# Value products by halves of the queries, placed after each of the two heads' scores

## The reference, cut to what matters

```
scores = jnp.einsum('bhqd,bhkd->bhqk', q, k) / SCALING
att = jax.nn.softmax(scores, axis=-1)
out = jnp.einsum('bhal,bhlv->bhav', att, v)
```

## Time and profile before

| | us |
|---|---|
| median of 3 runs (lowest, highest) | 983.62 (983.3, 984.05) |
| profiled execution, its own time | 983.9 |
| its span | 982.1 |
| TensorE busy with matmuls | 882.3 |
| VectorE busy | 792.7 |
| ScalarE busy | 663.7 |

### The profile page before, as it was taken

The page is one execution under the profiler, slowest core; times in us unless marked ns, Lnnn a source line. Parts: engine busy times, 40 slices in busy tenths (PEclk is TensorE's granted clock), DMA queues, the critical chain, the costliest instruction groups (busy, mean ns, idle before and its releaser), DMA issues. The chain is left out here.

```text
span 982.1 us, 14337 instructions
## 1 busy us (share of the span) xinstructions
PE 882.3 (90%) x5188; PEld 319.8 (33%) x5188; DVE 792.7 (81%) x1568; ACT 663.7 (68%) x728; POOL 314.5 (32%) x450
## 2 busy tenths in 40 slices
PE   6879999999999999999999999999989989757985
PEld 3312322222243233322332242322322313136863
DVE  4598879898979878899888879889799788265765
ACT  5128778787877787878877868788677768901110
POOL 4041010005424414139443423255243232822113
PEclk9769999999999999999999999999999989988998
DMA  5631010310320203101411022004310001240001
GB/s 143 105 45 39 16 53 16 73 41 10 90 61 13 93 12 70 38 13 55 89 61 56 12 39 59 23 7 105 91 56 14 11 13 31 85 172 23 1 1 64
DMA packets 52375, 49.08 MB, mean 50 GB/s; under 512 B 17504, under 2 KB 43696, under 8 KB 51920
## 3 DMA queue, kind: packets, MB, share of 16 engines
q1 hardware_dynamic: 51680, 46.91, 19.4%
q0 software_dynamic: 384, 1.05, 0.3%
q10 hardware_dynamic: 240, 0.20, 0.2%
HBM read 18.06 MB, written 9.17 MB: 28 GB/s over the span
## 5 line engine op out<-in xcount | busy, mean ns | idle before, releaser
L1331 DVE TENSOR_REDUCE mx<-ring 128x1 f32<-128x512 f32 x1024 | 633.9, 680 | 110.3 <-PE ring L1038 109.6
L873 ACT ACTIVATE prob<-sc,unscale 128x1024 f32<-128x1024 f32 x512 | 539.1, 1113 | 85.2 <-PE sc L1056 83.9
L1038 PE MATMUL ring<-kp,qp 48*128 48x512 f16 x1024 | 299.4, 395 | 43.5 <-DVE mx L1331 22.5
L1070 PE MATMUL obank<-prob,vaug 128*32 128x512 f32 x2048 | 276.1, 612 | 0.7 <-ACT prob L873 0.6
L1038 PEld LDWEIGHTS ring<-kp,qp 48*128 48x128 f16 x1024 | 74.1, 93 | 361.4 <-DVE mx L1331 301.3
L1056 PE MATMUL sc<-qp,kp 64*128 64x512 f16 x1024 | 167.9, 381 | 14.0 <-ACT prob L873 13.3
L644 POOL TENSOR_TENSOR parts<-qkf,parts 128x1024 f16<-128x1024 f32 x14 | 29.9, 2134 | 209.6 <-ACT parts L803 209.6
L1056 PEld LDWEIGHTS sc<-qp,kp 64*128 64x128 f16 x1024 | 50.4, 95 | 92.3 <-ACT prob L873 83.9
L631 POOL TENSOR_TENSOR hid<-hid,b 128x512 f32<-128x512 f32 x24 | 30.2, 1270 | 110.9 <-ACT hid L827 110.9
L639 POOL TENSOR_TENSOR yA<-yA,sums 128x512 f32<-128x512 f32 x15 | 19.0, 1269 | 131.1 <-DMA sums<-reciprocal_scratch 131.1
L1070 PEld LDWEIGHTS obank<-prob,vaug 128*32 128x32 f32 x2048 | 40.5, 108 | 61.5 <-issue 58.4
(11 more groups left out here) (221 smaller groups left out, 749.2 us busy)
## 6 DMA issues: line engine op xcount, KB each, us to landing
x_sb<-x SPq DMA_DIRECT2D x7, 1024.0 KB, 6.0
kp<-parts SPq DMA_DIRECT2D x48, 128.0 KB, 4.4
qp<-parts SPq DMA_DIRECT2D x93, 64.0 KB, 5.5
out<-hid SPq DMA_DIRECT2D x4, 1024.0 KB, 5.3
yA<-oT SPq DMA_DIRECT2D x124, 32.0 KB
sums<-reciprocal_scratch SPq DMA_DIRECT2D x31, 128.0 KB
x_scratch<-x SPq DMA_DIRECT2D x3, 1024.0 KB, 4.5
qp<-mp SPq DMA_DIRECT2D x128, 2.0 KB
```

What stands on the lines that cost most here:

```text
L873: nc.scalar.activation(prob[:, e % 2, 2 * a:2 * a + 2, :].rearrange("p g n -> p (g n)"), sbuf2[a][:, :], ACT.Exp, scale=unscale[:, 0:1]).t ...
L1038: nc.tensor.matmul(dst[:, :], qp[rows, qh, h, qt * P:(qt + 1) * P], kp[rows, h, kh * HALF:(kh + 1) * HALF], start=True, stop=True).then_in ...
L1070: ins = nc.tensor.matmul(obank[i * VW:(i + 1) * VW, :], vaug[:, b % 2, kt, c0:c0 + VW], prob[:, v % 2, i, :], start=(kt == 0), stop=(kt == ...
L1331: nc.vector.tensor_reduce(mx[:, u % 2, n:n + 1], src[:, :], AX.X, ALU.max).then_inc(rv_free, 1)
```

## The change

The value product is cut by query columns into two halves of 256. Each half is four heads' products with the same weights. Half 0 stands after scores(0), and scores(1) moves behind the second couple of max products, in front of half 1. The waits of the value product are on half 0, its signal `s_av` on half 1. The start flag of the bank is on half 0 of kt = 0 alone.

```
-                def value_product(v):
+                def value_product(v, half):
+
+                    cols = slice(half * HALF // 2, (half + 1) * HALF // 2)
...
-                    if kt == 0 and u > 0:
+                    if kt == 0 and u > 0 and half == 0:
                         pe.wait_ge(s_oT, u)
-                    if v % SL == 0:
+                    if v % SL == 0 and half == 0:
                         pe.wait_ge(ra_free, TAKEN["v", b, 3][1] + 1)
-                    pe.wait_ge(s_free, 2 * v + 2)
+                    if half == 0:
+                        pe.wait_ge(s_free, 2 * v + 2)
                     for i in range(GH):
                         c0 = (g * GH + i) * VS
-                        ins = nc.tensor.matmul(obank[i * VW:(i + 1) * VW, :], vaug[:, b % 2, kt, c0:c0 + VW],
-                                               prob[:, v % 2, i, :], start=(kt == 0), stop=(kt == NT - 1))
-                    ins.then_inc(s_av, 1)
+                        ins = nc.tensor.matmul(obank[i * VW:(i + 1) * VW, cols], vaug[:, b % 2, kt, c0:c0 + VW],
+                                               prob[:, v % 2, i, cols], start=(kt == 0 and half == 0),
+                                               stop=(kt == NT - 1), skip_group_check=True)
+                    if half == 1:
+                        ins.then_inc(s_av, 1)
...
                 if 0 <= e < NS:
                     scores(0)
-                    scores(1)
+                if 0 <= e - 1 < NS:
+                    value_product(e - 1, 0)
                 if e < 0:
                     items()
...
                 if t < NS:
                     max_products(range(2, 4))
+                if 0 <= e < NS:
+                    scores(1)
                 if 0 <= e - 1 < NS:
-                    value_product(e - 1)
+                    value_product(e - 1, 1)
```

## The result

The changed kernel takes 986.26 us (median of 14 runs, 984.52 to 987.97) against 983.88 us for the kernel before (14 runs, 983.3 to 986.9). The ratio is 1.0019, with a 95% interval of 1.0012 to 1.0027: slower, by 2.4 us, where 7.3 was forecast. The profiled execution has a time of 987.16 us and a span of 985.4 us.

The account below looks back on a forecast made before the run. VectorE was taken to bound plain slots, TensorE's path the gaps at items. Terms -10.7 + 9.1 + 4.6 + 2.4 + 1.9 = +7.3 us on 983.9 gave 991.2, forecast as 990.9 us; range 978 to 1010.

Parts of the forecast that it names:

- So VectorE bounds a plain slot: Slots without items: VectorE's four gapless reductions take 2.49 us and set the slot; TensorE and ScalarE have some room.
- Plain slots, cost about nothing: Slots without items: the new order of waits fits within VectorE's 2.49 us with 0.04 to spare, so no time lost.
- the ring from T to T: Loop from one step's second exponential's end to the next's, through half 0, max products and scores(1): 2.45 us.
- Slots with items: From a slot's last max product to the next slot's items, 1.30 us becomes 1.09: 51 slots gain 0.21 each, -10.7 us.
- V0 in such a slot takes time in which TensorE waited for VectorE anyway: In slots with items, half 0 costs nothing: 1.49 us were there for 1.05 of streams and loads.
- Late T: Second exponential ending over 0.12 us late holds up half 0, max products, VectorE: +9.1 evacuations, +4.6 qk, +2.4 z and u.
- Evacuations and qk items: ScalarE's value-bank evacuations and qk work delay half 0: 0.38 us lost in 24 and 12 slots, +9.1 and +4.6 us.
- The slack of 0.12: In a plain slot, the third max product is ready 0.12 us before VectorE reaches it, so smaller delays cost nothing.
- The end: Last 12 slots, without max products between: 2.01 us becomes 2.24 each, 2.8 us, of which 0.9 hidden: +1.9 us.
- faster: late T doesn't reach VectorE: Rival: larger slack before VectorE's reduction absorbs the delays of the second exponential; 975 us in the full case; chance 0.16.
- the ring binds every slot: Rival: half 0 costs above 0.61 us, so the loop between second exponentials exceeds 2.49; 1004 to 1020 us; chance 0.16.
- Bound by the number of instructions: Rival: eight short products cost as much as eight long, a half 0.99 us; above 1050 us; chance 0.03.

Follow-up runs that it names:

- e4: Kernel before, with value products of key tiles 1 to 7 over the first 256 query columns only: 965.94 us, one execution.
- e10: Kernel before, with every maximum taken over 384 of the 512 columns of its bank: 949.11 us, one execution.
- e11: Changed kernel, with every maximum taken over 384 of the 512 columns of its bank: 964.83 us, one execution.
- e7: Kernel before, run once more unchanged to see the scatter between executions: 983.65 us.
- e3: Changed kernel, halves apart only where slots seemed to gain: not at first key tile, with z, u, x, behind qk, or after the last max product: 977.34 us.
- e2: Changed kernel, but with the old order (both halves at the slot's end) at the first key tile of a unit: 977.75 us, ratio 0.9936.
- e1: Changed kernel, but both halves together at the slot's end and scores(1) directly behind scores(0): 984.84 us, ratio 1.0009.
- e9: e2, but cut at the first key tile with p or w items, and whole with z or u items and behind qk: 974.26 us, ratio 0.9903.

## Why the prediction was right and wrong

**The step that failed: "So VectorE bounds a plain slot", and with it "Plain slots, cost about nothing".** The 24 reductions without a gap were taken as an engine at its limit. The rows already held the other answer. In the kernel before: value product 463.01 to the next M0 at 464.00 is 0.99; M0's load to its reduction 0.43; the reduction 0.68; its end, 465.11, to M3's load at 465.18, 0.07, for M3 takes the bank that M0 filled; M3 to the next value product 0.31. The sum is 2.48 us, the slot. TensorE and VectorE wait for each other once a slot, and VectorE's wait is invisible, because the records of reductions overlap: 0.68 us long, they start every 0.599 when nothing holds them (changed kernel), and 0.622 looked just as closed. Asked for in narrow windows, VectorE's timeline of the kernel before shows where in the slot the wait is:

```profile
464.43 0.69 DVE L1331 TENSOR_REDUCE mx<-ring 128x1 f32<-128x512 f32 x1
465.64 0.68 DVE L1331 TENSOR_REDUCE mx<-ring 128x1 f32<-128x512 f32 x1
466.24 0.68 DVE L1331 TENSOR_REDUCE mx<-ring 128x1 f32<-128x512 f32 x1
466.92 0.69 DVE L1331 TENSOR_REDUCE mx<-ring 128x1 f32<-128x512 f32 x1
```

(One reduction, between the first two lines, isn't shown.) The starts are 0.60 to 0.61 apart, but 0.68 ahead of M0's reduction (466.24 to 466.92), which waits for M0. VectorE's own limit is 4 x 0.599 = 2.39. e4 (less TensorE work, slot 2.39) and e10 (one shorter reduction, slot shorter by one reduction's part) show both.

The change takes 0.21 us out of this ring, the same 1.30 - 0.21 = 1.09 that the prediction credited to slots with items alone. The ring falls to 2.27 and the slot to the next limits, VectorE's 2.39 and the ring from T to T, which measures 0.05 + 0.57 + 0.65 + 1.11 = 2.38 (load of M2 at 472.87, exponential at 473.52, so 0.65 where 0.72 was taken). e11 shows that this ring alone would hold 2.39. So 89 of the 150 plain slots gained 0.10 each, and with the other slots without items that is **-9 us** (e7) to -11 (profiled execution) against a forecast of 0. The prediction's view was right for the 58 slots at kt 2 and 3 alone: there VectorE has its small work besides, bounds the slot in both kernels, and the change gains next to nothing.

**Slots with items.** -0.21 a slot was exact for the 24 with h, p, w or qk. It was half that for the 12 that also have mt, and in slots with u, x or z there was a loss of 0.05 to 0.32 in place of a gain. Forecast -10.7 for 51 slots, and +2.4 for what z and u delay. Measured, -6.2 for the first two kinds, and +3.6 for u, x, z and mt alone (+3.8 by e7). The step "V0 in such a slot takes time in which TensorE waited for VectorE anyway" fails in a slot with u, where the loss is 0.32 (changed kernel):

```profile
616.25 0.16 PEld L1073 LDWEIGHTS obank<-prob,vaug 128*32 128x32 f32 x8 [0.43 <-issue]
...
616.82 0.10 PEld L1038 LDWEIGHTS ring<-kp,qp 48*128 48x128 f16 x2 [0.41 <-issue]
...
617.25 0.69 DVE L1339 TENSOR_REDUCE mx<-ring 128x1 f32<-128x512 f32 x1 [0.22 <-PE ring L1038]
```

V0 holds up M2, and VectorE stands idle for 0.22 until M2 is ready.

What holds the u, x and z slots was not tried by itself: in the old order, between slots of the new one, those with mt are still 3.76 (e3) against 3.57 to 3.60 before, while those without mt are back at their old length. So V0's place is the loss in slots without mt and a part of it in those with mt; for the rest no cause was found. (The prediction's term for z and u is 9 x 0.28 = 2.5, not 2.4.)

**Late T.** Evacuations and qk items: forecast 9.1 + 4.6 = 13.7, measured 10.8 + 3.2 = 14.0. The mechanism and the number of slots were right, and e2 removed the evacuations' part. The slack of 0.12 was not: it was worked out from a pace of 0.622. In a plain slot of the changed kernel M2 is ready at 467.60 + 0.43 = 468.03, and its reduction starts at 463.25 + 8 x 0.599 = 468.04, so the slack is 0.01. A slot behind an evacuation is 0.49 longer than the new plain slot (2.88 against 2.39), so nearly the whole delay of 0.50 is lost. It comes to the forecast 0.38 only against the old 2.49: two errors of 0.1, in the slack and in the plain slot, cancel, and that the sum came out is luck. VectorE's gap shows 0.39 for the same reason as above, since the overlap of the records hides 0.08. The three slots with both lose 0.84, 0.10 more than the sum of the two (0.39 + 0.35).

**The end.** 2.17 us a slot, not 2.24 (the scores' load to the exponential is shorter than taken): +1.5 with 1.1 hidden, +0.4 net, where +1.9 was forecast.

**Balance,** against e7: 7.3 - 9.1 (plain slots) + 4.5 (items credited too much) + 1.4 (u, x, z, mt) + 0.3 (late T) - 1.5 (end) = 2.9 us, measured 2.4. The sign was right, the sum off by a plain-slot term of -9 and item terms of +6 that cancel two thirds of it. So that the sign came out right is luck too: with the item terms as forecast the kernel would have been faster. Of the rivals, "faster: late T doesn't reach VectorE" fell (it does, by 0.39); "the ring binds every slot" had the right ring but the wrong sign, since what it was compared with, 2.49, was no limit of VectorE. "Bound by the number of instructions" fell in e1: sixteen products take 1.00 us where eight of twice the columns took 0.99, and the slot didn't move. The Trainium skill (TensorE: Matmul & The Clock Gate, "Wait — 56ns, not 53.3ns?") gives some 62 ns per matmul with hardware decode off; by an estimate from that figure sixteen products would take at least 0.99 us. e1's 1.00 doesn't exclude it, nor does the 0.57 of a half exclude 8 x 62 ns = 0.50, but neither shows it, since the columns' time fits both.

## What to carry to other kernels

A stretch of records without a gap doesn't prove an engine at its limit: compare the pace with the fastest pace of the same instruction anywhere, and add up the loops of waits through it; if such a loop's sum equals the slot, the loop is the bound. What shortens one slot's critical stretch shortens every slot that is held by the same loop, so a gain found in special slots has to be tried on the plain ones. A reordering that gains in most slots and loses in a few known ones is worth applying slot by slot: here the old order in 42 of 242 slots turned +0.2% into -1.0% (e9). But neighbours are coupled: a slot's gain has to be counted together with the slots behind it.

## What the runs showed of the hardware

- Reductions of 128x512 out of the banks have records of 0.68 us and start every 0.599 us when fed. The Trainium skill (VectorE: DVE Perf Modes, "The DRAIN you can't avoid") says that the next operation starts once the pipeline has emptied, and earlier if nothing holds it. Here the records of neighbours overlap by 0.08 us, and a wait of about that size (0.68 from start to start instead of 0.60) shows as no gap.
- Products of 128 partitions, four side by side, took 0.57 us for eight of 256 columns (load to the load of what follows), 1.00 for sixteen of 256 and 0.99 for eight of 512. So cutting them costs nothing while the halves stand together, and 0.15 (2 x 0.57 - 0.99) when they stand apart.
- TensorE's clock fell to the half level in short stretches after it had stood waiting for VectorE's statistics. In the kernel before, then in its second execution (windows: us, busy of PE, PEld, DVE, ACT, POOL, clock, DMA share, GB/s):

```profile
712.00:722.00 10.00, 9.05 (x53) 2.06 (x57) 9.06 (x17) 6.49 (x8) 9.26 (x19) 0.83 0.05 15
784.00:798.00 14.00, 10.78 (x58) 2.25 (x57) 11.48 (x26) 7.48 (x9) 7.98 (x19) 0.76 0.03 11
```

```profile
712.00:722.00 10.00, 8.21 (x60) 2.12 (x56) 9.95 (x21) 6.68 (x8) 7.09 (x18) 1.00 0.05 15
784.00:798.00 14.00, 10.52 (x63) 2.34 (x61) 12.74 (x29) 8.57 (x9) 7.42 (x19) 0.88 0.03 11
```

  TensorE had waited 1.81 us for a bank at the first stretch in both executions (until 712.67 and 714.93), and its clock fell to the half level, with a value product of 1.86 us in place of 1.06, in one alone. At the second it had waited 3.4 us in both, and the clock fell in both. The profiled execution is 2.3 us longer than the second one over the slots, as much as the whole change: a comparison of two single profiles would have put it down to the order of the products.
